# Four banks for turned scores, three for scores, and bank waits at their own products in a 16-head attention

## The reference, cut to what matters

```python
def _L1_attn_ref(x, Wqkv, Wo):            # x: (8, 512, 256), H = 16, DH = 16
    qkv = x @ Wqkv.T
    q, k, v = jnp.split(qkv, 3, axis=-1)  # then to (b, H, t, DH)
    q = cos * q + rotate_half(q) * sin
    k = cos * k + rotate_half(k) * sin
    scores = jnp.einsum('bhqd,bhkd->bhqk', q, k) / math.sqrt(DH)
    scores = jnp.where(causal, scores, -jnp.inf)
    attn = jax.nn.softmax(scores, axis=-1)
    out = jnp.einsum('bhqk,bhkd->bhqd', attn, v)
    return out.transpose(0, 2, 1, 3).reshape(b, t, d) @ Wo.T
...
x = x + _L1_attn_ref(_layernorm(x, axis=-1), L1_attn_Wqkv, L1_attn_Wo)
```

## Time and profile before

| what | before |
| --- | --- |
| median of 3 runs (lowest, highest) | 2533.52 us (2532.68, 2536.14) |
| the profiled execution: time, span | 2531.52 us, 2529.8 us |
| TensorE busy, share of the span | 2267.8 us, 90% |
| VectorE, ScalarE, GpSimd busy | 62%, 52%, 36% |
| loop of the first pair, S0 to the last part 2 | 648.6 to 739.6 us |
| tails of pairs 0 to 3, T0 of chunk 6 to L1375 | 23.8, 23.8, 23.8, 21.3 us |

### The profile page before, as it was taken

The page is one execution under the profiler, slowest core; times in us unless marked ns, Lnnn a source line. Parts: engine busy times, 40 slices in busy tenths (PEclk is TensorE's granted clock), DMA queues, the critical chain, the costliest instruction groups (busy, mean ns, idle before and its releaser), DMA issues.

```text
span 2529.8 us, 45343 instructions
## 1 busy us (share of the span) xinstructions
PE 2267.8 (90%) x15874; PEld 1748.3 (69%) x15874; DVE 1555.9 (62%) x4796; ACT 1315.7 (52%) x3214; POOL 922.6 (36%) x1363
## 2 busy tenths in 40 slices
PE   7999599996778788877699999999999999999998
PEld 5777499994445363544567777777777777777777
DVE  6665422224666757565667676777777667776675
ACT  2221133333555755465555675666755675656753
POOL 2221122213434433332543344333544445343451
PEclk9999699998787988878899999999999999999999
DMA  3222411112001010100200000000101000000000
GB/s 132 100 100 90 130 36 37 39 30 79 19 10 59 3 59 11 35 35 11 88 9 18 16 3 18 18 18 10 44 26 62 19 9 26 26 26 18 10 18 26
DMA packets 75937, 96.41 MB, mean 38 GB/s; under 512 B 6113, under 2 KB 69090, under 8 KB 75458
## 3 DMA queue, kind: packets, MB, share of 16 engines
q1 hardware_dynamic: 70786, 81.89, 9.7%
q0 software_dynamic: 3408, 9.31, 1.3%
q10 hardware_dynamic: 1520, 2.31, 0.3%
HBM read 62.69 MB, written 30.28 MB: 37 GB/s over the span
## 4 chain that ended last, share of the span: by engine, by line
PE 27%; DVE 9%; ACT 8%; issue 5%; POOL 3%; DMA 0%; SPq 0%; DVEq 0%; POOLq 0%; ACTq 0%
PE l_free L2194 4%; PE l_free L2196 4%; PE l_free L2195 3%; PE l_out L2309 3%; PE l_score L2269 2%; POOL l_probs L1684 2%; PE l_turned L2290 2%; DVE l_probsT L1779 2%; DVE l_work L1856 2%; PE l_turned L2194 1%; PE l_turned L2196 1%; PE l_turned L2195 1%; DVE l_u_low L1862 1%; ACT l_probs L2068 1%; PE l_turned L2243 1%
## 5 line engine op out<-in xcount | busy, mean ns | idle before, releaser
L1684 POOL TENSOR_SCALAR l_probs<-l_probs,l_rinv 128x256 f32<-128x256 f32 (+1 forms) x512 | 223.5, 456 | 227.6 <-DVE l_rinv L1839 227.5
L1114 DVE CUSTOM_DVE_ANT_0 c_raw<-cbank,c_later 128x256 f32<-128x256 f32 (+3 forms) x512 | 218.3, 487 | 73.3 <-PE cbank L1301 73.0
L2068 ACT ACTIVATE l_probs<-l_probs,l_nmax 128x256 f32<-128x256 f32 (+1 forms) x512 | 239.9, 473 | 26.5 <-DVE l_nmax L1834 26.4
L1217 ACT ACTIVATE c_cprobsT<-cbank 128x384 f32<-128x384 f32 (+1 forms) x384 | 180.9, 525 | 95.8 <-PE cbank L1327 95.7
L1834 DVE CUSTOM_DVE_ANT_0 l_probs<-l_score,mask,l_inv 128x256 f32<-128x256 f32 (+1 forms) x512 | 200.0, 447 | 28.8 <-PE l_score L2269 28.1
L2194 PE MATMUL l_free<-l_part,l_w_high 128*128 128x512 f32 x384 | 166.4, 433 | 9.6 <-DVE l_probsT L1779 6.6
L2194 PE MATMUL l_free<-l_wqkv_high,l_yT 128*128 128x512 f32 x384 | 159.0, 414 | 1.9 <-DVE l_part L1758 1.9
L1817 DVE COPY l_probsT<-l_turned 128x512 f32<-128x512 f32 (+1 forms) x128 | 79.9, 624 | 131.3 <-PE l_turned L2290 80.3
L1006 POOL TENSOR_SCALAR_AFFINE_SELECT c_cprobsT<-c_cprobsT 128x256 f32<-128x256 f32 x256 | 99.6, 413 | 154.3 <-ACT c_cprobsT L1217 152.2
L2196 PE MATMUL l_free<-l_part,l_w_low 128*128 128x512 f32 x384 | 153.0, 398 | 0.0
L2195 PE MATMUL l_free<-l_yT,l_w_high 128*128 128x512 f32 x384 | 152.8, 398 | 0.0
(11 more groups left out here) (282 smaller groups left out, 5932.1 us busy)
## 6 DMA issues: line engine op xcount, KB each, us to landing
w<-in_W1T SPq DMA_DIRECT2D x8, 1024.0 KB, 8.0
w<-in_W2T SPq DMA_DIRECT2D x8, 1024.0 KB, 11.8
ys_d<-m_y SPq DMA_DIRECT2D x39, 128.0 KB, 1.7
xn_d<-a_prods SPq DMA_DIRECT2D x8, 512.0 KB, 3.6
c_came<-x_d SPq DMA_DIRECT2D x8, 512.0 KB, 4.9
y_d<-c_raw SPq DMA_DIRECT2D x8, 512.0 KB, 3.7
early_rows<-y_d SPq DMA_DIRECT2D x8, 512.0 KB, 3.7
l_came<-y_d SPq DMA_DIRECT2D x8, 512.0 KB, 3.9
```

The lines of the kernel that those rows point to most:

```text
L1114: last = dve.tensor_tensor_reduce(raw[:, CHUNKS - NS + s, h * 2 * P:h * 2 * P + wide], score_place("scores", u, s)[:, h * 2 * P:h * 2 * P ...
L1217: act.activation(probsT[s][:, c % 2, i, k0:k0 + w], turned_place(j, s)[:, 0:w], ACT.Exp).then_inc(probs_ready[s], 1)
L1684: pool.tensor_scalar(a, a, rinv[:, j, r, h:h + 1], 1.0, ALU.mult, ALU.mult).then_inc(normed, 1)
L2068: act.activation(a, a, ACT.Exp, bias=nmax[:, j, r, h:h + 1], scale=-1.0, accum_out=rsum[:, j % 2, r, h:h + 1])\
```

## The change

`score_bank` becomes `bank[0][0..2]` and `turned_bank` becomes `bank[0][3]` with `bank[1][0..2]`. The numbers of places in `score_place`, `turned_place`, `free_place` and in the wait on `probs_ready` follow. The waits for a bank move from ahead of both streams to the first product of the stream that they are for. For pairs after the first, `row_measure(1)` comes before `row_norm(0)` on VectorE. Part 0 of the output of the last chunk comes one step later on TensorE, after T4 of that chunk instead of after T3.

```diff
-        score_bank, turned_bank, sum_bank = bank[0], bank[1][0:3], bank[1][3]
+        score_bank, turned_bank, sum_bank = bank[0][0:3], [bank[0][3]] + bank[1][0:3], bank[1][3]
...
-            return score_bank[rotation.index((what, u, s)) % 4]
+            return score_bank[rotation.index((what, u, s)) % 3]
...
-            return turned_bank[(NS * j + s) % 3]
+            return turned_bank[(NS * j + s) % 4]
...
                         whole_rows(1)
-                        row_norm(0)
-                        row_measure(1)
+                        if trip:
+                            row_measure(1)
+                            row_norm(0)
+                        else:
+                            row_norm(0)
+                            row_measure(1)
                         row_norm(1)
...
-                        if n >= 4:
-                            was, v, r = rotation[n - 4]
+                        if n >= 3:
+                            was, v, r = rotation[n - 3]
...
-                        for s in range(NS):
-                            if u == 0:
+                        if u == 0:
+                            for s in range(NS):
                                 pe.wait_ge(qkT_ready[s], pair * (4 * NT) + 4 * NT)
                                 pe.wait_ge(v_ready[s], pair * NT + NT)
-                            free_place("scores", u, s)
                         wide = max(2, qt + 1) * P
                         for i in range(n):
                             for s in range(NS):
+                                if i == 0:
+                                    free_place("scores", u, s)
...
-                        for s in range(NS):
-                            if j % PER_CHUNK == 0:
+                        if j % PER_CHUNK == 0:
+                            for s in range(NS):
                                 pe.wait_ge(nmax_rows[c % 2][s], pair * (16 * CHUNKS) + 32 * (c // 2 + 1))
-                            m = NS * j + s - 3
-                            if m >= 0:
-                                pe.wait_ge(probs_ready[m % NS], pair * UNITS + m // NS + 1)
                         for kt in kts:
...
                             for s in range(NS):
+                                m = NS * j + s - 4
+                                if kt == kts[0] and m >= 0:
+                                    pe.wait_ge(probs_ready[m % NS], pair * UNITS + m // NS + 1)
...
                         for part in range(3):
-                            if j >= 3 and (j - 3 - 2 * part) % PER_CHUNK == 0 and 0 <= j - 3 - 2 * part < UNITS:
+                            if part == 0 and u == UNITS + SCORE_LAG - 3:
+                                continue
+                            if part == 0 and u == UNITS + SCORE_LAG - 2:
+                                output(CHUNKS - 1, part)
+                            elif j >= 3 and (j - 3 - 2 * part) % PER_CHUNK == 0 and 0 <= j - 3 - 2 * part < UNITS:
```

## The result

| what | before | changed |
| --- | --- | --- |
| median of 5 runs (lowest, highest) | 2534.34 us (2532.68, 2537.66) | 2518.16 us (2514.50, 2527.57) |
| ratio of the changed to the one before, 95% interval | | 0.9941 [0.9918, 0.9964] |
| the profiled execution: time, span | 2531.52, 2529.8 | 2527.57, 2525.8 |
| loops of the four pairs, first scores to L1375 (changed: L1384), added up | 362.6 us | 360.7 us |

The account below looks back on a forecast made before the run. The steady stretch was taken as bound by the hand-over of banks, the tail by one queue's order. Head +3.6, steady stretch 0 and tail -14 gave -10.4 us, so 2523 us, range 2512 to 2533.

Parts of the forecast that it names:

- The steady stretch: About 20 chunks in four pairs, 8.35 to 8.75 us each against 8.53: -4 to +4 us, taken as 0.
- S5 to T1 ... 0.50 to 0.44 less: In a steady chunk, T1 follows the half of S0 left: 1.25 to 1.31 us after S5, today 1.75.
- the forecast's ledger: Sum of a chunk's pieces from S1 to the next S1: 8.35 to 8.75 us, against 8.53.
- the forecast's balance of the two: Between S3 and T5, stream 1's new wait at S4 takes the place of T5's 0.43 us wait.
- What the turned side gains the score side pays: Steady stretch: time saved by four turned banks is lost to waits with three score banks; net 0 us.
- The forecast's 0.94 us of waits on the turned side: Waits at T5 (0.43) and T1 (0.51) for an exponential go with four turned banks, if nothing replaces them.
- The head: Scores alone, VectorE full: T0 delayed 0.6 to 1.3 us a pair, taken as 0.9; +3.6 us (2.4 to 5.2).
- The tail: End of each pair: `row_measure(1)` fills VectorE's wait, bans come earlier; 12.7 to 22.2 us saved, taken as 14.
- O0 stands behind T4: In the tail, part 0 of the last chunk's output comes after T4, so O0 covers T5's 0.67 us wait.
- Rival 1: Steady stretch: the flip's longer wait isn't given back, +0.6 us a chunk; total +1.6, 2535 us; chance 0.09.
- Rival 2: Waits between two streams' products delay the second in 384 places; at 0.1 us each 2561 us; chance 0.05.
- Rival 3: The tail doesn't shorten if the clock falls before T0; saves 1 to 2 us a pair, 2532; chance 0.12.

Follow-up runs that it names:

- the experiment with waits ahead: The changed kernel, but all waits of a step stand ahead of both streams' first products again; ratio to the kernel before 1.0087.
- the second measurement: The changed kernel measured once more with nothing altered, against the kernel before on the same chip; ratio 0.9961.

## Why the prediction was right, and where it wasn't

**Size and sign.** Forecast -10.4 us and 2523; measured 2518.2, and 2522.9 when the kernel ran again. By the loops the three terms are +2.1, +3.8 and -18.5, -12.6 together, and none came at its forecast of +3.6, 0 and -14. That their sum came within 2.2 us is luck in part, since the errors make up for each other. The late rises of the clock, up to 10.8 us in a profile, stand in no term.

**The steady stretch** (forecast 0, -4 to +4; 8.35 to 8.75 a chunk). Measured 8.72, so 20 x 0.19 = +3.8, the upper edge. Term by term: S1 to F 1.90 (forecast 1.90), F to S3 1.72 (1.71), S3 to T5 1.32 (1.30 to 1.40), T5 to S5 1.22 (1.09 to 1.21), S5 to S1 2.56 (2.35 to 2.53). S1 to F and S0's second product came to the hundredth, though F's wait came as 0.44 inside S2 and 0.18 at F, and not as 1.0 in one piece. What failed in the sum is "S5 to T1 ... 0.50 to 0.44 less" with the piece behind it: S0's second product starts at 1.10 as reckoned, but O2 comes 0.66 after T1's first product and not 0.3 to 0.44: T1's first starts beside S0's second (both at 685.01), and its second 0.34 later and not beside its first.

**What sets the way from F to T0** was missed by the forecast's ledger, which fills it with the waits at S4 and T5. T0 needs the maxima that F turned, by ScalarE's copy and the DMAs. The rows of the chunk in the kernel before (F at 694.58), of its tail (where T0 at 724.70 is marked as waiting for that DMA), of the changed kernel (F at 679.64), and of the changed kernel with the flip behind T3 (F at 677.72):

```profile
695.64 2.38 SPq L939 DMA_DIRECT2D c_cqT<-c_nmaxT  x4
699.36 0.50 PE L1327 MATMUL cbank<-c_cqT,c_ckT 64*128 64x512 f32 x2
```

```profile
720.97 2.38 SPq L939 DMA_DIRECT2D c_cqT<-c_nmaxT  x4
```

```profile
680.71 2.38 SPq L939 DMA_DIRECT2D c_cqT<-c_nmaxT  x4
684.28 0.50 PE L1332 MATMUL cbank<-c_cqT,c_ckT 64*128 64x512 f32 x2
```

```profile
678.79 2.38 SPq L939 DMA_DIRECT2D c_cqT<-c_nmaxT  x4
682.35 0.51 PE L1332 MATMUL cbank<-c_cqT,c_ckT 64*128 64x512 f32 x2 [0.25 <-issue]
```

From the end of the last DMA's issue (695.64 + 2.38 = 698.02) to T0 it is 1.34 us in the steady stretch before and 1.35 in the tail before; in the two others it is 1.19 and 1.18. The same holds in all profiles here at the full clock: by the median T0 comes 4.79 or 4.80 behind F with the waits ahead (three profiles) and 4.64 or 4.65 with own waits (eleven), with three or four banks on either side, and whether S5 starts 3.8 or 4.3 behind F. So by these rows this chain sets that half of the chunk, though TensorE isn't marked idle before T0 in most of them; no run shortens the chain to test it. Then neither the 0.43 at T5 nor the new wait of 0.31 at S4 is in the chunk's time, and the forecast's balance of the two came out right by luck. The sum by the two halves is 4.79 + 2.46 + 1.29 = 8.54 before and 4.64 + 2.18 + 1.90 = 8.72 changed (F to T0, T0 to S1, S1 to F). Why own waits make the first term 0.15 shorter isn't shown.

**The step that was wrong in kind** is "What the turned side gains the score side pays". It put the gain down to the fourth turned bank and treated the place of the waits as a cost only. The experiments give one path of three parts for a chunk: own waits -0.24 (8.53 to 8.29, old banks), three score banks instead of four +0.61 (8.29 to 8.90), the fourth turned bank -0.18 (8.90 to 8.72). In another order the shares differ: with the new banks own waits give -0.18 (8.90 to 8.72). For T0: own waits -0.5, the missing score bank +1.0, the turned bank nothing. So the trade of banks costs 0.43 x 20 + 1.0 x 4 = 12.7 us by these parts, and the kernels with and without it stand 17 to 22 apart. The forecast's 0.94 us of waits on the turned side did go, but the place of the waits alone removes half of them (0.22 + 0.22 are left with the old banks), and only those at T1 were on the path.

**The head** (forecast +3.6) came to (15.33 - 14.80) x 4 = +2.1. The place was right: F comes 10.39 after the first scores against 9.95, and T0 5.00 behind F in both. The price was too high, since the same own waits shorten the head by 0.5, which the sum left out. VectorE ran dry for 0.20 us once.

**The tail** (forecast -14, 12.7 to 22.2) came to 3 x 5.2 + 2.9 = -18.5. The forecast put it to the power's order and the later part. These two edits are worth 8.4 us with the old banks and waits and 8.6 with the new; the other 10 come with the banks and own waits alone, 3.8 of them in the last pair. The power's order is the cause of 2.5 to 2.9 us in each of pairs 0 to 2, shown by leaving it out. T0 of the last chunk came 0.4 earlier (726.96 - 719.14 = 7.8 against 8.3; forecast 0.2). The clock enters too: the forecast's mean of 0.69 is that of the second pair, the four tails before have 0.79, 0.69, 0.70 and 0.78, and the changed ones 0.84, 0.91, 0.84 and 0.91. What was said of the later part ("O0 stands behind T4", taken as needed) is wrong: the bans are early enough without it, and it costs 0.3 us a tail at the full clock. It helps while the bans are late: without the order on VectorE, 22.0 with the old place and 21.2 with the new. That isn't all of it, since with the old banks and the flip behind T3 the tails are 22.2 and 22.0 with the old place and 21.4 with the new, though the bans are early in both. What settles it there is open.

**The rivals.** Rival 1 (flip's wait not given back) came true to a third, 0.19 of 0.6. Rival 2 (parted pairs) is excluded as a net loss by the experiment with waits ahead. By the Trainium skill (TensorE: Matmul & The Clock Gate, "The mechanism") matmuls start and end in program order. The trace agrees: T1's first product, whose bank is free, starts at 685.01, 1.11 after S5, where S0's second is let go at 1.10. Rival 3 (the clock in the tail) came true in single tails: with the clock down within 1 us of T0 of the last chunk, the fourth tail of the second measurement gained 1.6 us, and three with the tail's edits alone 2.3, 2.3 and nothing. The clock cost more in another place, the second chunk of some pairs, with 5.4 us each, which no rival had.

**Open.** When the clock rises in a pair's first chunks differs from pair to pair and run to run of the same kernel (10.0 to 10.4 or 13.1 us for that chunk), and so does its fall in the tail. What sets either wasn't tried. The ratios of single kernels carry some 5 us of it.

## What to carry to other kernels

When two streams share a queue, put each wait at the product that needs it before moving banks: here that alone was worth 0.24 us of 8.53 a chunk and 0.5 us a head, while the exchange of a score bank for a turned one cost 0.43 a chunk on top. Before a wait is counted as gain, see whether another chain sets the same stretch: here the way from F to T0 kept its length to 0.01 us while the waits inside it came and went. A bank taken from a pool whose reader is nearly always busy (VectorE, 6.8 us of 8.5) cost one reader's step, 0.61, at the flip. A short operation of one queue (a power of 1 us) that stands ahead of another chain's work held that chain by 2.5 us and more a tail; ask what it waits for, and let its producer go first.

## What the runs showed of the hardware that was not expected

A product that waits in the queue holds back the next one also when that one's bank is free, but the product ahead of it runs on: S4 of the changed kernel has one of its four products 0.59 us before the other three, though the third goes into the same bank as the first. And less idle time didn't bring the higher clock sooner: in the changed kernel's second pair TensorE was busy all of 7.4 us from T0 on and stayed at 1.2 GHz for some 16 us after that. In the same pair of the kernel before it was busy 6.27 of 6.9 us, and the clock stood at 2.4 GHz from there on. Granted clock in the windows of the two kernels, the changed one first:

```profile
810.60:818.00 7.40, 7.40 (x30) 3.64 (x32) 3.49 (x12) 4.38 (x9) 2.03 (x6) 0.50 0.01 3
```

```profile
812.10:819.00 6.90, 6.27 (x26) 2.38 (x26) 3.86 (x14) 4.50 (x9) 2.04 (x6) 0.50 0.00 1
819.00:864.60 45.60, 38.24 (x370) 19.27 (x367) 36.64 (x172) 34.26 (x74) 18.18 (x52) 1.00 0.01 4
```
